# A decoder layer on one core: keys of a quad in 128+128+52, the summed weights one turn later, the first pair's splits between the residuals, the bias adds in the up half

## The reference

```
x1 = x  + S5(norm(x))                   # state-space recurrence, 64 states
x2 = x1 + attention(norm(x1), ctx)      # 16 heads of 32, ctx of 4 x 77 x 512
y  = x2 + FFN(norm(x2))                 # 512 -> 2048 -> gelu -> 2048 -> 512
```

## Time and profile before

| | us |
|---|---|
| median of 3 runs | 2468.38 (2464.81 to 2469.06) |
| the profiled execution | 2464.39 |
| its span | 2462.6 |
| a plain attention turn | 47.2 |
| an FFN pair | 170 |

### The profile page before, as it was taken

One profiled execution on the slowest core, in us unless ns is written; L12 is line 12 of the kernel. 1 busy time (PEld: TensorE's weight loads), 2 busy tenths in 40 slices (PEclk: granted clock), 3 DMA queues, 4 the chain that ended last, 5 costly groups with the idle time before them and its releaser, 6 DMA issues.

```text
span 2462.6 us, 42345 instructions
## 1 busy us (share of the span) xinstructions
PE 2267.3 (92%) x15816; PEld 1972.6 (80%) x15816; DVE 1810.6 (74%) x2969; ACT 1293.4 (53%) x2832; POOL 582.8 (24%) x618
## 2 busy tenths in 40 slices
PE   8877789999999999869989899899899899998998
PEld 4777577777777777748988888889889889888898
DVE  4999668777778777745876857957858768678567
ACT  3997565656566666533634535535435345354343
POOL 3777222222222222210030210200300302102103
PEclk9888889999999999979999999999999999999999
DMA  8554613322332332236657576576676576675765
GB/s 327 190 181 172 235 40 112 108 84 80 106 118 74 102 104 75 90 141 216 205 167 253 186 232 207 184 255 183 188 257 186 179 262 195 216 216 177 222 189 179
DMA packets 189115, 424.25 MB, mean 172 GB/s; under 512 B 25574, under 2 KB 62950, under 8 KB 188518
## 3 DMA queue, kind: packets, MB, share of 16 engines
q1 hardware_dynamic: 188928, 421.73, 53.1%
HBM read 331.08 MB, written 90.60 MB: 171 GB/s over the span
## 4 chain that ended last, share of the span: by engine, by line
PE 69%; DVE 13%; ACT 9%; issue 4%; DMA 3%; POOL 1%; DVEq 0%; SPq 0%; ACTq 0%; POOLq 0%
PE ps L411 55%; PE ps L1771 6%; ACT es L970 3%; PE ps L1740 2%; DMA xa<-in_x 2%; DVE st L1131 1%; DVE rawx L1304 1%; PE ps L1751 1%; DVE ptl L1160 1%; DVE gl L1160 1%; ACT pth L945 1%; DMA x_scratch<-xa 1%; PE ps L1704 1%; DVE xtl L1160 1%; DVE wc_s L1160 1%
## 5 line engine op out<-in xcount | busy, mean ns | idle before, releaser
L411 PE MATMUL ps<-ring,gh 128*128 128x256 f32 x3584 | 665.4, 287 | 46.5 <-DVE gl L1160 45.8
L411 PEld LDWEIGHTS ps<-ring,gh 128*128 128x128 f32 x3584 | 563.9, 194 | 55.6 <-DVE gl L1160 34.6
L411 PE MATMUL ps<-xth,ring 128*128 128x512 f32 x1792 | 559.4, 392 | 18.9 <-ACT U L1050 12.6
L411 PE MATMUL ps<-ring,gl 128*128 128x256 f32 x1792 | 510.6, 285 | 0.0
L411 PEld LDWEIGHTS ps<-xth,ring 128*128 128x128 f32 x1792 | 338.6, 189 | 93.7 <-issue 18.5
L1040 ACT ACTIVATE gh<-G 128x512 fp32r<-128x512 f32 x384 | 235.3, 628 | 224.8 <-PE ps L411 224.8
L1160 DVE TENSOR_TENSOR gl<-G,gh 128x512 fp32r<-128x512 f32 x384 | 303.2, 799 | 67.1 <-ACT gh L1040 66.6
L411 PE MATMUL ps<-xtl,ring 128*128 128x512 f32 x896 | 350.6, 391 | 0.0
L411 PEld LDWEIGHTS ps<-ring,gl 128*128 128x128 f32 x1792 | 347.2, 194 | 0.0
L748 POOL TENSOR_TENSOR es<-es,rinv 128x308 f32<-128x308 f32 x256 | 180.7, 737 | 512.7 <-DVE rinv L1380 512.7
L1440 DVE TENSOR_TENSOR U<-ps,U 128x512 f32<-128x512 f32 (+1 forms) x168 | 137.2, 817 | 166.8 <-PE ps L411 157.5
(11 more groups left out here) (205 smaller groups left out, 4572.9 us busy)
## 6 DMA issues: line engine op xcount, KB each, us to landing
ring<-wup_scratch SPq DMA_DIRECT2D x224, 512.0 KB, 3.6
ring<-wdn_scratch SPq DMA_DIRECT2D x224, 512.0 KB, 3.6
X<-x_scratch SPq DMA_DIRECT2D x32, 1024.0 KB, 8.3
xa<-in_x SPq DMA_DIRECT2D x16, 1024.0 KB, 5.3
x_scratch<-xa SPq DMA_DIRECT2D x16, 1024.0 KB, 4.3
x<-x_scratch SPq DMA_DIRECT2D x16, 1024.0 KB, 5.6
x_scratch<-x SPq DMA_DIRECT2D x16, 1024.0 KB, 4.3
out_x<-X SPq DMA_DIRECT2D x16, 1024.0 KB, 6.3
```

Source lines behind the costliest of these rows:

```text
L411: mm = pe.matmul(bank, a, b, start=first and i == 0, stop=last and i == n - 1, skip_group_check=go_on)
```

## The change

- The keys of a quad are cut in 128, 128 and 52. The high and low parts of the third chunk lie in one tile, `pt2`, at partitions 0 and 64 up; the rows of V for it are loaded at both places. So the third chunk takes one pass with `vh` and one with `vl`: 8 matmuls. POOL zeroes `pt2` once, in turn 0. `load_v` has 14 pieces for 12.
- Turn g makes the weights' chunk g-1 (the last in turn 16), and with other places: `mix_weights` before the second row sums, `high_weights` after the last value part, `low_weights` where it was.
- The first pair's statistics, normalization, transposes and splits move: statistics from turn 15 to 16; five of the seven splits into turn 16 between the residuals, the last two into turn 17. The table for gelu is loaded in turn 16.
- For pairs 0 to 6 the bias is added after the down sums, that is during the next pair's up half, before the store of the output. U's quarters are swapped, so that the first up chunk uses those that are free first. The statistics of the next x run in chunks 4 to 7 instead of 3 to 6, the second normalization at down unit 4, and the splits at other units.

```diff
-    KP = (CK + 2) // 3
-    CKP = 3 * KP
-    NJ = KC * 3
-    V_AT = [0, 2 * HD, 5 * HD, 9 * HD]
+    KT = CK - 2 * P
+    KB = P // 2
+    KU = KB + 2
+    CKP = 2 * P + KU
+    VW = [2 * HD, HPC * HD, HPC * HD]
+    V_AT = [0, VW[0], VW[0] + VW[1], sum(VW)]
+    assert 2 * L <= P + L and 2 * P < CK <= 2 * P + KB
...
-    pth = r2.put("pth", [KP, NJ, GT], F32R)
-    ptl = r2.put("ptl", [KP, NJ, GT], F32R)
+    pth = r2.put("pth", [P, 2 * KC, GT], F32R)
+    ptl = r2.put("ptl", [P, 2 * KC, GT], F32R)
+    pt2 = r2.put("pt2", [P, KC, GT], F32R)
...
-        X_MIX_AT = 26, 29, 32, 34
-        X_HI_AT = 26, 27, 30, 31, 32, 34, 36
-        X_LO_AT = 27, 30, 33, 36, 38, 41, 43
+        X_MIX_AT = 24, 28, 32, 37
+        X_HI_AT = 25, 27, 30, 33, 35, 38, 40
+        X_LO_AT = 26, 30, 34, 39, 42, 46, 48
...
             while r < L:
-                c, at = divmod(h * L + r, KP)
-                n = min(L - r, KP - at)
-                pieces.append((h, r, n, c, at))
+                c, at = divmod(h * L + r, P)
+                n = min(L - r, P - at)
+                pieces += [(h, r, n, c, at)] + [(h, r, n, c, at + KB)] * (c == 2)
                 r += n
-        assert [(h, c) for h, _, _, c, _ in pieces] == [(0, 0), (1, 0), (1, 1), (2, 1), (2, 2), (3, 2)]
...
             load_wc(0)
-            for n in range(2):
-                store_wc(n)
-                load_wc(n + 1)
+            store_wc(0)
+            load_wc(1)
...
                 turn(g)
-                store_wc(g)
-                load_wc(g + 1)
...
+            store_wc(NG - 3)
+            load_wc(NG - 2)
+            store_x2(NG - 1)
...
             load_wc(NG - 1)
-            store_x2(NG - 1)
+            store_x2(NG)
             store_wc(NG - 1)
-            store_x2(NG)
...
                     sp.wait_ge(x_added, 2 * p + 2)
+                    sp.wait_ge(xr_ready, 2 * p + i + 1)
...
-                    if b == 3 and p:
+                    if b == 6 and p:
                         store_out(p - 1)
-                    if b == 7 and p < NP - 1:
+                    if b == 10 and p < NP - 1:
...
                     rsqrt(NG + 1 + g, xn2_ready, g + 1)
+                if g == 0:
+                    for j in (2, 3):
+                        pool.wait_ge(fold_stored[j], 16 * 2)
+                    nc.gpsimd.memset(pt2[:, :, :].bitcast(F32), 0.0).then_inc(p_zero, 1)
...
-                        rsqrt(2 * NG, xn2_ready, NG)
 
...
-                pool.wait_ge(xr_ready, 2 * p + i + 1)
+                pool.wait_ge(xr_loaded, 32 * p + 32)
+                if p == NP - 1:
+                    pool.wait_ge(xr_ready, 2 * p + i + 1)
...
-                bias(p, 0)
-                bias(p, 1)
+                else:
+                    bias(p, 0)
+                    bias(p, 1)
...
                 add_x(p, 1, 2, 0, DN_21)
+                if p < NP - 1:
+                    pool.wait_ge(x_added, 2 * p + 2)
+                    bias(p, 0)
+                    pool.wait_ge(x_last, p + 1)
+                    bias(p, 1)
 
...
-                if g == NG + 1:
-                    act.wait_ge(x2_stored, 16 * (NG - 2))
-                    act.wait_ge(wc_stored, 32 * NG)
-                    for o in SPLIT_ORDER:
-                        hi_x3(0, o)
-
...
                     if has(d):
-                        for q in range(3):
-                            hi(pth[:, 4 * q:4 * q + 4, t * P:(t + 1) * P], P_SLOT[t] + q)
+                        for q, part in ((0, pth[:, 0:KC]), (1, pth[:, KC:2 * KC]), (2, pt2[0:KT])):
+                            hi(part[:, :, t * P:(t + 1) * P], P_SLOT[t] + q)
...
                 if g == NG:
-                    apply3(1)
+                    load_table(ACT.Gelu)
+                    apply3(0)
...
                 hi_x(0)
+                if g == NG:
+                    apply3(1)
...
                 hi_x(1)
-                if g == NG:
-                    for i in range(4):
-                        raw_x(0, i, i)
...
                 hi_v(3)
+                if 1 <= g <= NG:
+                    high_weights(g - 1)
                 if g == NG:
-                    for i in range(4):
-                        raw_x(0, 4 + i, i)
+                    for i in range(8):
+                        raw_x(0, i, i % 4)
+                    act.wait_ge(x2_stored, 16 * (NG - 2))
+                    act.wait_ge(wc_stored, 32 * NG)
+                    for o in SPLIT_ORDER:
+                        hi_x3(0, o)
...
                         act.wait_ge(fold_stored[j], 16 * 2)
+                    act.wait_ge(p_zero, 1)
...
                 hi_p(1, 0)
-                if g == NG - 1:
-                    apply3(0)
                 exp(3)
-                if g < NG:
-                    high_weights(g)
...
                     hi_q(o)
...
                         act.wait_ge(up_sum, summed(p, c - 2, SUM_12))
+                    elif c:
+                        after(act, x_last, p)
                     else:
-                        after(act, x_last, p)
-                    A(U[:, c % 2], ps[:, 4 * (c % 2) + UP_BANK[A11], :], ACT.Copy).then_inc(first_copied, 1)
+                        after(act, x_added, 2 * p)
+                    A(U[:, 2 - 2 * (c % 2)], ps[:, 4 * (c % 2) + UP_BANK[A11], :], ACT.Copy).then_inc(first_copied, 1)
...
                         for e in range(GR):
...
-                        apply3(2 * p + 2 + (c == 7))
+                    if more and c == 6:
+                        apply3(2 * p + 2)
...
                     hi_g(p, e)
+                    if more and e == GR:
...
 
+            def split_first(a, b):
+                for o in SPLIT_ORDER[a:b]:
+                    if MIX_BEFORE[o]:
+                        mix_x(0, MIX_BEFORE[o] - 1)
+                    lo_x3(0, o)
...
                     if has(d):
-                        for q in range(3):
-                            part = lambda w: w[:, 4 * q:4 * q + 4, t * P:(t + 1) * P]
-                            lo(part(ptl), part(pth), P_SLOT[t] + q)
+                        for q, part, high in ((0, ptl[:, 0:KC], pth[:, 0:KC]), (1, ptl[:, KC:2 * KC], pth[:, KC:2 * KC]),
+                                              (2, pt2[KB:KB + KT], pt2[0:KT])):
+                            tok = slice(t * P, (t + 1) * P)
+                            lo(part[:, :, tok], high[:, :, tok], P_SLOT[t] + q)
 
...
                 residual(2, -2)
+                if g == NG:
+                    stats3(0)
...
                 residual(3, -2)
+                if g == NG:
+                    stats3(1)
                 if g == NG + 1:
-                    for o in SPLIT_ORDER:
-                        if MIX_BEFORE[o]:
-                            mix_x(0, MIX_BEFORE[o] - 1)
-                        lo_x3(0, o)
+                    split_first(5, PROD)
...
                 lo_x(0)
+                if 1 <= g <= NG:
+                    mix_weights(g - 1)
...
                 lo_v(3)
-                if g == NG - 1:
-                    stats3(0)
-                if g < NG:
-                    mix_weights(g)
+                if g == NG:
+                    low_weights(g - 1, 0)
+                    low_weights(g - 1, 1)
...
                         dve.wait_ge(fold_stored[j], 16 * 2)
+                    dve.wait_ge(p_zero, 1)
...
                 sums(2)
-                if g == NG - 1:
-                    stats3(1)
                 lo_x(3)
+                if g == NG:
+                    split_first(0, 3)
                 residual(1, -1)
+                if g == NG:
+                    split_first(3, 5)
...
                 lo_q(0)
-                if g < NG:
-                    low_weights(g, 0)
+                if 1 <= g < NG:
+                    low_weights(g - 1, 0)
                 sums(3)
-                if g < NG:
-                    low_weights(g, 1)
+                if 1 <= g < NG:
+                    low_weights(g - 1, 1)
...
                     spread2(g + 2, range(0, 2))
...
                 elif i == DN_11:
-                    dve.wait_ge(xr_ready, 2 * p + 1)
+                    dve.wait_ge(xr_loaded, 32 * p + 32)
...
                     b = lambda j: ps[:, 4 * (c % 2) + UP_BANK[j], :]
-                    u2, u3 = U[:, c % 2], U[:, 2 + c % 2]
+                    u2, u3 = U[:, 2 - 2 * (c % 2)], U[:, 3 - 2 * (c % 2)]
...
                         dve.wait_ge(x2_stored, 16 * (NG - 2))
-                    tiles = [2 * (c - 3) + i for i in range(2)] if more and 3 <= c < 7 else []
+                    tiles = [2 * (c - 4) + i for i in range(2)] if more and 4 <= c else []
                     early, late = tiles[0:1], tiles[1:2]
...
                     if p and c < 2:
-                        dve.wait_ge(x_added, 2 * p)
+                        dve.wait_ge(*((x_last, p) if c else (x_added, 2 * p)))
...
                         for j in range(4):
-                            f, c = divmod(4 * q + j, 3)
```

(20 more changed lines are left out.)

22 lines of the change are left out of this document (14 added, 8 removed).

## The result

The changed kernel takes 2367.24 us (median of 4 runs, 2365.58 to 2368.68), the kernel before on the same chip 2466.65 us (4 runs, 2464.81 to 2469.06): ratio 0.9596, 95% interval 0.958 to 0.9613. The forecast was 2383 (2356 to 2424), a gain of 81.5 us where 99 came. The profiled execution took 2366.6 us, its span 2364.8.

What follows compares the result with a forecast made beforehand. TensorE was taken as the bound in attention turns, VectorE slowed by GpSimd in the FFN down half. Gains of 29.8 (attention) + 14 (change of stage) + 37.7 (FFN) = 81.5 us gave 2383, range 2356 to 2424.

Steps and rivals of the forecast that it cites:

- Bias into the up half: FFN: moving GpSimd's bias adds out of the down half ends VectorE's doubled operations there; net -37.7 us.
- The 45.8 us go: FFN down half: TensorE's 45.8 us of waits for VectorE's low parts vanish, except 0.7 us; counted as -45.
- the price of the late statistic: Last up chunk: last statistic and moments delay the second low part, so down unit 1 waits; 1.65 x 7 = 11.5 us lost.
- Weights one turn later: Attention turn's end: high copy moved to the middle lets the project start earlier; 1.4 us in turns 1 to 13, plus 0.1.
- Keys: Attention values product: 64 matmuls fewer at 0.231 us, 14.8 us (0.92 per turn); batch changes take back 2.7.
- Change of stage: From attention to FFN: values start earlier and the copy into U comes at 1091; gain 14 us, bounds 5 and 20.
- 1 (the middle copy): Attention: ScalarE's high copy in mid-turn becomes the gate and each turn gets back 1.7 us; 2425, chance 0.12.
- 2: Change of stage gains nothing, because the last weights' store gates the splits longer; 2397, chance 0.12.
- 3: FFN: VectorE stays late in the down half from the splits' new places, 45.8 remains; 2428, chance 0.08.
- 4: FFN up half: doubled VectorE operations follow the bias and stall chunks 0 and 1, 23 us; 2406, chance 0.08.
- 6: FFN: adds slip back into the down half, so the slow operations stay where they are; 2430, chance 0.02.
- 5: Attention: the single weight buffer's load lands after the mixing's new place; slower than before, e.g. 2480, chance 0.03.

Runs made afterwards that it cites:

- old_places: Changed kernel with the mixing and the splits of the next pair's x back at the earlier kernel's down units, bias still in the up half: 2367.84 us, 0.9604.
- old_keys: Changed kernel with the old key chunks again, weight work, first pair's splits and bias staying in their new places: 2375.47 us, 0.9634.
- bias_back: Changed kernel with the bias adds and their waits back at the start of each down half, new places of mixing and splits kept: 2401.45 us, 0.9744.
- after_no_bias: Changed kernel with each bias add cut from 512 columns to one, so bias is left out but for column 0: 2364.84 us, 0.9597.

## Why the prediction was right, and where it was not

*Bias into the up half* had the right mechanism and a mis-sized term. The step "The 45.8 us go" holds (0.2 us left without the bias), and so does the price of the late statistic: 12.5 us of waits remain where 11.5 and 0.7 were forecast. What failed is the equation of wait rows with time: "-45 - 4.2 + 11.5 = -37.7" is a sum of rows. Measured: 55.3, of which 37.6 are waits (50.1 to 12.5). The clock's sum fell by 12.6 (16.3 to 3.7), and old_places puts some 5 us on the new places. That 37.6, 12.6 and 5 add up to 55.3 is in part luck, since the clock's sum is an upper bound. The pairs before at full clock show what the rows left out: VectorE's lateness costs 7.4 to 7.6 us a pair whether TensorE waits it out at full clock (6.8 to 7.3 us in rows) or runs part of it slowly (6.2). How much of the 12.6 is clock that the changed kernel would have paid at the same waits stays open. The Trainium skill ("TensorE: Matmul & The Clock Gate", Part 1) says that the clock follows how busy TensorE has recently been; the windows above agree in that, among the pairs shown, the clock falls only where TensorE has waited, but the same three waits left it up in the pair from 1496. I had read "full clock" in one plain turn and asked no further.

*Weights one turn later* was forecast at 1.4 + 0.1 us a turn; old_keys against the kernel before gives 47.20 - 45.27 = 1.9. The mechanism held, the size was short by a quarter.

*Keys* was forecast at 0.92 us a turn by itself. The passes' price held (sixteen take 3.71 us, 0.232 each), its place did not: alone the cut brings 0.5 us in a plain turn, and less than nothing after clock and loads; behind the moved weights 0.68. The step "what it does counts" was wrong while ql ended last. I had seen 2.35 us of gaps in the turn and costed the keys as if they shrank with the work. The sum came out by luck (2.6 a plain turn, 2.4 forecast): one error went against the other, the batch turns took back 5.7 us (three of 51.0, 51.6 and 47.6 became 50.5, 48.5 and 49.2: 3 x 2.6 less 2.1), not 2.7, and three turns that the lowered clock made 48.8 us long are plain ones after, 1.6 us more each.

*Change of stage*: U's copy was forecast at 1091 in before's time; its matmuls came 42.5 us earlier than before where 43.8 had been forecast in all, but 9.5 of that came in this stretch and not 15 (the 14, and the 1.0 for turn 14). Two steps erred: turn 15 lost 2.85 us to a store of 13.21 us queued behind the x loads, which "SP stores after the low parts as before" passed over; and the projection stood 12.5 us behind the splits, "three residuals of 0.7 and a project of 2.8 now between them", which I had counted as work and not as a queue: from the landing of the store (1036.90) to U's matmuls it took 25.7 us, where 22.5 had been forecast. The working has a gap too: the terms named for the earlier start of values add up to 10.9 us, not 12, and the step from there to 13.6 isn't given.

Rivals: 1 (the middle copy) is out, since ptl waits are 2.8 us in 13, less than before's 6.9; 2 is out, 9.5 us were gained; 3, 4 and 6 by bias_back and after_no_bias; 5 by the plain turns. On rival 4 the Trainium skill ("SBUF — State Buffer", Who interferes with whom) says that the port pair VectorE and GpSimd share is an exclusive lock, and that the order of issue, not the shape of the operation, decides which of them blocks. The traces agree in that both get longer: VectorE's mix 1.22 to 2.32 us, and GpSimd's add of 512 columns 17.56/8 = 2.2 us beside it, 5.37/4 = 1.3 in the up half.

## What to carry to other kernels

A wait row is not the price of the wait: that was 1.2 (all FFN waits) to 1.8 times the row (batch changes) here. Read the granted clock of the windows behind it, and ask which engine sets the pace there: where TensorE does, a lowered clock comes on top of the wait; where the late engine does, as VectorE in before's pairs, it seems to take the wait's place. Before you credit work taken off the busiest engine, find what ends last in that loop: the same 64 matmuls were worth nothing, and some 8 us once the end of the turn was free. When a long step is moved in an in-order queue, list what stands behind it at its new place; four reorderings of that kind, with no work removed, gave 37 us by the medians, 35 by the ratios.

## What was not expected of the hardware

- Behind three waits in a row, none over 2.3 us, the granted clock fell (0.63 in the window from 1415); behind the same three in the next pair (1575 to 1583) it stayed at 1.00, and of bias_back's first seven pairs, all with the same waits for the down half, six have a lowered clock there and one has not. In the changed kernel's pair from 1344, with one wait of 1.6 us, every window is at 1.00.
- A bias add of one column still takes 5.67/8 = 0.7 us on GpSimd, against 1.3 for 512 columns undisturbed.
- A store issued right behind two loads of 1 MB took 13.21 us, and at most 8.2 us when issued ahead of them.
